# Message layer of a graph network: five of sixteen edge tiles gathered by TensorE instead of three, from a table in two fp16 parts

## The chip, the core and the metric

One NeuronCore of one Trainium2 chip runs the whole program. The metric is the device time in microseconds, the median of three runs. Work is spread over TensorE (PE), VectorE (DVE), ScalarE (ACT), GpSimd (POOL) and the queue of SyncE (SP), which only issues transfers.

## What is computed

Four graph layers over 3125 nodes of 96 features and 100,000 edges, with a layer norm before each later one. The change lies in the third, the message layer:

```python
src = edge_index[0]
dst = edge_index[1]
msg = jax.nn.relu(x[src] + edge_attr)
aggr = jax.ops.segment_sum(msg, dst, num_segments=x.shape[0])
h = x + aggr
h = jax.nn.relu(h @ W1 + b1) @ W2 + b2
return x + jax.nn.relu(h)
```

Edges are sorted by `dst`, and `edge_attr` here is an array of 100,000 x 96 floats. The first two layers work with a dense matrix of edge counts, the fourth (gated) layer gathers rows of 192 features for every edge.

## The kernel before

Edges are cut into tiles of 128 (`EP`), eight tiles (`GT`) to a group, 98 groups (`NG`). Node rows are held as 25 blocks (`NT`) of 125 nodes (`NP`). `message_layer` (L837) writes a program for each engine; the loops over groups are unrolled in it, and the engines meet at semaphores.

For each group the layer needs the 1024 source rows `x[src]` of 96 floats. They come in two ways.

- *By DMA.* POOL issues one indirect DMA for a tile (L931), which reads 128 rows of 384 bytes from the table `h_rows` into one of seven buffers (`RING`). It waits on `rows_free`, which DVE raises at the end of `make_onehots`.
- *By TensorE.* `picked_tiles` (L792) names the tiles that are left to it: one of an even group and two of an odd one, three of the sixteen of a pair. For such a tile DVE compares the 128 source ids, held in PSUM as f32 on 125 partitions, with the number of each node: one instruction of 25 x 128 elements (`make_picks`, L1007) makes a 0/1 matrix in bf16. `gather_rows` (L1130) multiplies it, in 25 matmuls that add up in PSUM, with the table `parts`, where each row of `h` stands as three bf16 parts (288 columns). `take_rows` (L1013) sums the three parts into the group's buffer. SP loads the ids (`load_row`), and ACT turns them into f32 (`widen`, L943).

When a group's rows are there, DVE adds the edge attributes, which SP loads into a ring of seven buffers (`add_edges`, L1036). ACT applies the ReLU in place (L958). DVE compares the destination ids with a stretch of 64 node numbers (`make_onehots`, L1057), and TensorE multiplies the eight tiles with these one-hot matrices in f32 (L1145). DVE adds the result to `aggT` (`add_total`, L1045). `group_steps` reads how many stretches a group has from a table that the kernel makes; there are 99 for the 98 groups.

The order on each engine is written out by hand. DVE, for a group g: `take_rows(g)`, `add_edges(g)`, `make_onehots(g)`, `make_picks(g + 2)`. TensorE: the sums of g, then `gather_rows(g + 2)`. ACT: the ReLU of g and, after an odd group, `widen` for the pair after next. SP: the edges of g and, after an even group, a row of ids for the pair after next. The gated layer (`gated_layer`, L1204) runs after it, with its own buffers and 784 indirect DMAs (L1269).

## Time and profile before

| | us |
|---|---|
| median of 3 runs | 3581.68 (3578.87 to 3584.29) |
| span of the profiled execution | 4069.9 |
| the profiled execution's own time | not given beside its span |
| message layer's loop in the profile | about 1600 to 2665 |
| gated layer's loop in the profile | about 2773 to 3963 |

Busy time over the span: PE 2792.4 us (69%), weight loads 1983.6 (49%), DVE 2233.5 (55%), POOL 1439.0 (35%), ACT 678.5 (17%). Times in the profile are us from the span's start; the span is 14% longer than the time of the runs. A group of lines gives busy time, the mean duration of one instruction in ns, and the idle time of the engine in front of it with what ended it; "issue" is idle time in which it waited for nothing that the profile shows, "remote" a releaser that it can't name.

### The profile page before, as it was taken

To read this page: it belongs to the slowest core of one execution; us is meant where nothing else is said; L and a number is where in the kernel's file an instruction comes from. 1 tells how busy PE (TensorE), PEld (TensorE's weight loads), DVE (VectorE), ACT (ScalarE), POOL (GpSimd) and SP (SyncE) were. 2 spreads that over 40 slices of the span, in tenths; PEclk is the share of its full clock that TensorE was granted. 3 is DMA by queue.
4 is the path that set the end of the run, shared out by engine and by line. 5 is a ranking of instruction groups with operands and counts; after the bars stand their busy time and mean duration, and the time that the engine had idled before them with its cause. 6 is when DMAs were issued, how large, how long until landed. Compare 5 with 4: busy or idle time off the path is not lost.

```text
span 4069.9 us, 59352 instructions
## 1 busy us (share of the span) xinstructions
PE 2792.4 (69%) x19895; PEld 1983.6 (49%) x19896; DVE 2233.5 (55%) x3813; ACT 678.5 (17%) x1120; POOL 1439.0 (35%) x1447
## 2 busy tenths in 40 slices
PE   3677779999998997577777777774244544454555
PEld 1211128999997775355555555552133323333333
DVE  6887777333346336476676676672244444444446
ACT  0234554000004001010010010011011111111111
POOL 0000000000000002565665665615566666667660
PEclk9999997999998998677777787775577666666766
DMA  0000000000000002222232232303222222222220
GB/s 24 0 0 0 0 0 3 2 2 2 2 2 4 1 1 54 64 78 72 76 78 74 73 78 75 84 12 85 66 79 75 75 76 74 73 74 78 75 73 16
DMA packets 109268, 180.96 MB, mean 44 GB/s; under 512 B 38949, under 2 KB 73287, under 8 KB 109049
## 3 DMA queue, kind: packets, MB, share of 16 engines
q0 software_dynamic: 58016, 108.47, 10.5%
q1 hardware_dynamic: 51033, 69.40, 6.1%
q8 instruction: 158, 2.59, 0.3%
q14 instruction: 61, 0.50, 0.0%
HBM read 172.96 MB, written 4.80 MB: 44 GB/s over the span
## 4 chain that ended last, share of the span: by engine, by line
PE 16%; another core or an unknown queue 15%; DVE 15%; issue 10%; ACT 1%; POOL 1%; DVEq 1%; DMA 1%; POOLq 0%
PE msg_sums L1130 10%; DVE msg_pick L1007 4%; PE msg_sums L1145 3%; DVE gate_rows L1331 3%; DVE gate_gated L1337 2%; DVE gate_gate L1340 1%; DVE gate_onehot L1365 1%; PE gate_sums L1429 1%; PE gate_sums L1440 1%; POOL gate_rows L1269 1%; DVE msg_rows L1036 1%; DVE msg_rows L1013 1%; DVE pre_aggT L1348 0%; DVEq L1356 0%
## 5 line engine op out<-in xcount | busy, mean ns | idle before, releaser
L1269 POOL DMA_INDIRECT gate_rows<-first_rows,all_src_i x784 | 774.7, 988 | 420.9 <-issue 232.0
L931 POOL DMA_INDIRECT msg_rows<-h_rows,all_src_i x637 | 642.7, 1009 | 423.6 <-DVEq L1060 247.6
L1130 PE MATMUL msg_sums<-msg_parts,msg_pick 125*128 125x288 bf16 x3675 | 622.9, 326 | 147.2 <-issue 133.9
L1440 PE MATMUL gate_sums<-gate_onehot,gate_passed 128*97 128x64 f32 x1584 | 223.9, 299 | 568.0 <-DVE gate_onehot L1367 290.4
L1130 PEld LDWEIGHTS msg_sums<-msg_parts,msg_pick 125*128 125x128 bf16 x3675 | 394.2, 111 | 351.3 <-issue 210.4
L919 POOL IOTA msg_node_no<- 125x25 f32 x1 | 0.2, 162 | 1588.9 <-POOLq L642 1588.9
L1331 DVE TENSOR_TENSOR gate_rows<-gate_rows,gate_sums 128x1536 f32<-128x1536 f32 x98 | 171.7, 1752 | 677.1 <-remote 500.4
L572 PE MATMUL hop_sums<-dense_work,dense_counts 125*128 125x192 f16 x6250 | 521.8, 247 | 14.3 <-DVE dense_t L526 6.6
L572 PEld LDWEIGHTS hop_sums<-dense_work,dense_counts 125*128 125x128 f16 x6250 | 519.1, 98 | 16.9 <-DVE dense_t L526 7.2
L1440 PEld LDWEIGHTS gate_sums<-gate_onehot,gate_passed 128*97 128x97 f32 x1584 | 206.9, 215 | 643.1 <-DVE gate_onehot L1367 354.9
L1007 DVE TENSOR_TENSOR msg_pick<-msg_sums,msg_node_no 125x3200 bf16<-125x3200 f32 x147 | 507.9, 3483 | 0.6 <-ACT msg_sums L943 0.3
L1429 PE MATMUL gate_sums<-pre_we,gate_edge 128*128 128x256 f32 (+1 forms) x784 | 373.5, 615 | 103.9 <-issue 94.1
L415 PE MATMUL cnt_sums<-cnt_hot,cnt_near 128*128 x1000 | 344.8, 406 | 121.4 <-DVE cnt_hot L354 116.4
L1145 PE MATMUL msg_sums<-msg_onehot,msg_rows 128*96 128x64 f32 x1584 | 224.2, 291 | 128.2 <-issue 120.6
L1429 PEld LDWEIGHTS gate_sums<-pre_we,gate_edge 128*128 128x128 f32 x784 | 181.8, 243 | 228.3 <-issue 209.3
L1145 PEld LDWEIGHTS msg_sums<-msg_onehot,msg_rows 128*96 128x96 f32 x1584 | 203.9, 205 | 159.8 <-issue 153.0
L415 PEld LDWEIGHTS cnt_sums<-cnt_hot,cnt_near 128*128 x1000 | 97.3, 97 | 363.3 <-issue 356.9
L1291 ACT ACTIVATE gate_gated<-gate_rows 128x768 f32<-128x768 f32 x98 | 82.7, 844 | 1018.7 <-DVE gate_rows L1331 603.1
L958 ACT ACTIVATE msg_rows<-msg_rows 128x768 f32<-128x768 f32 x98 | 82.6, 843 | 992.7 <-DVE msg_rows L1036 641.6
L352 DVE TENSOR_TENSOR cnt_near<-dense_work,cnt_src_n 128x256 f16 x500 | 180.3, 361 | 112.0 <-issue 87.9
L779 PE MATMUL conv_sums<-dense_work,dense_counts 125*128 125x288 bf16 x1875 | 236.3, 290 | 7.9 <-DVE dense_t L708 7.9
L1013 DVE TENSOR_REDUCE msg_rows<-msg_sums 128x96 f32<-128x288 f32 x147 | 64.5, 452 | 285.6 <-remote 273.6
(240 smaller groups left out, 2829.6 us busy)
## 6 DMA issues: line engine op xcount, KB each, us to landing
msg_edge<-edges SPq DMA_DIRECT2D x98, 384.0 KB
gate_edge<-edges SPq DMA_DIRECT2D x98, 128.0 KB
gate_rows<-first_rows,all_src_i POOLq DMA_INDIRECT x784
msg_rows<-h_rows,all_src_i POOLq DMA_INDIRECT x637
msg_src_row<-src_rows SPq DMA_DIRECT2D x49, 187.5 KB
first_rows<-pre_first SPq DMA_DIRECT2D x6, 375.0 KB
all_x<-x SPq DMA_DIRECT2D x1, 1171.9 KB
h_rows<-all_h SPq DMA_DIRECT2D x6, 187.5 KB
```

The lines of the kernel that those rows point to most:

```text
L352: nc.vector.tensor_tensor(nears.rearrange("p (c i) -> p c i", i=2), pairs2, low, ALU.is_equal)
L415: end_of_pair = nc.tensor.matmul(sums[:, b, 0:WIN * NT], nears.rearrange("p (c i) -> p i c", i=2)[:, i, :], hots[i], start=False, stop=Tru ...
L572: last = nc.tensor.matmul(sums[:, g0 + i, 0:2 * D], counts[0:NP, at:at + 128], half[frm][:, k, :], start=(k == 0), stop=(k == NT - 1))
L779: last = nc.tensor.matmul(sums[:, 4 * (q % 2) + i, 0:3 * D], counts[0:NP, at:at + 128], parts[:, j, :], start=(j == 0), stop=(j == NT - 1))
L931: nc.gpsimd.indirect_dma_start(out=rows[:, r, k, :], out_offset=None, in_=table, in_offset=bass.IndirectOffsetOnAxis(ap=src_i[:, at:at + 1 ...
L1007: nc.vector.tensor_tensor(pick[:, i % WIDE, :, :], source, spread(node_no[:, :], EP), ALU.is_equal).then_inc(picked, 1)
L1130: last = nc.tensor.matmul(got_rows[i % WIDE], pick[:, i % WIDE, j, :], parts[:, j, :], start=(j == 0), stop=(j == NT - 1))
L1145: last = nc.tensor.matmul(total[group % LAG], rows[:, group % RING, k, :], onehot[:, group % LAG, k, :], start=(k == 0), stop=(k == GT - 1))
L1269: nc.gpsimd.indirect_dma_start(out=rows[:, r, k, :], out_offset=None, in_=table, in_offset=bass.IndirectOffsetOnAxis(ap=src_i[:, at:at + 1 ...
L1331: nc.vector.tensor_tensor(to, to, products, ALU.add).then_inc(added, 1)
L1429: last = nc.tensor.matmul(sums[:, bank, to:to + end - frm], edge[:, group % SLOTS, half, :], we[:, frm:end], start=True, stop=True)
L1440: last = nc.tensor.matmul(total[group % LAG], passed[:, group % KEPT, k, :], onehot[:, group % LAG, k, :], start=(k == 0), stop=(k == GT - 1))
```

## The change

Five tiles of a pair are left to TensorE, two of the even group and three of the odd one. The ids are shifted by 1600 and kept in SBUF as fp16 (`src_near`), so that whole numbers up to 3125 fit exactly. The picks of a pair are made by 25 TENSOR_SCALAR instructions, one for each block of nodes, each for all 5 x 128 ids: 16 of them after an odd group, nine after the next even one. A pick is 1/4096 instead of 1, and the table holds two fp16 parts of 4096 h (192 columns). `take_rows` is gone: `add_edges` adds the edge attributes to the first part in PSUM, then to the tiles that came by DMA, then the second part. The edge ring has four buffers instead of seven. The picks share one space with `hT` and `first`, which are used after the loop, and with two tiles of the gated layer. On the host the table of ids is cut for five tiles.

```diff
-WIDE = 3
+PICKED = 5
+FIRST_HALF = 16
+EDGES = 4
+ROW_LIFT = 4096.0
+MIDDLE = 1600.0
...
@@ -792,8 +796,12 @@
 
 def picked_tiles(group):
 
-    first = group // 2 * WIDE
-    return [(first, GT - 1)] if group % 2 == 0 else [(first + 1, GT - 2), (first + 2, GT - 1)]
+    return [(0, GT - 2), (1, GT - 1)] if group % 2 == 0 else [(2, GT - 3), (3, GT - 2), (4, GT - 1)]
+
+
+def tiles_picked(groups):
+
+    return groups // 2 * PICKED + groups % 2 * 2
 
...
-        self.hT = m.sb("hT", [D, N], F32)
-        self.first = m.sb("first", [NP, 2, 4, 2 * D], F32)
+        space = m.sb("space", [EP, NT * PICKED * EP], F32)
+        self.pick = space[0:NP, :].bitcast(F16).rearrange("p (s t e) -> p s t e", s=2, t=NT)
+        self.hT = space[0:D, 0:N]
+        self.first = space[0:NP, 3136:3136 + 2 * 4 * 2 * D].rearrange("p (i n d) -> p i n d", i=2, n=4)
+        self.room = space[:, 4736:NT * PICKED * EP]
...
+        dst_f, iota, hT, first, pick = pre.dst_f, pre.iota, pre.hT, pre.first, pre.pick
...
-        edge = m.sb("edge", [EP, RING, GT, D], F32)
...
-        pick = m.sb("pick", [NP, WIDE, NT, EP], BF16)
-        parts = m.sb("parts", [NP, NT, 3 * D], BF16)
-        src_row = m.sb("src_row", [NP, 2, WIDE * EP], I32)
+        parts = m.sb("parts", [NP, NT, 2 * D], F16)
+        src_row = m.sb("src_row", [NP, 2, PICKED * EP], I32)
+        src_near = m.sb("src_near", [NP, 2, PICKED * EP], F16)
+        shift = m.sb("shift", [NP, 1], F32)
...
-        hid = m.sb("hid", [D, 2, 4 * NP], F32)
+        both = m.sb("both", [EP, 2 * 4 * NP], F32)
+        hid = both[0:D, :].rearrange("p (i w) -> p i w", i=2)
+        dst_i = both[:, 0:ET].bitcast(I32)
...
-        got_rows = [sums[:, 2 + i, 0:3 * D] for i in range(WIDE)]
-        wide = [sums[0:NP, b, 0:WIDE * EP] for b in (6, 7)]
+        got = [sums[:, 2, :].rearrange("p (i w) -> p i w", w=256),
+               sums[:, 3:5, :].rearrange("p b (i w) -> p (b i) w", w=256)]
...
-                r = group % RING
-                if group >= RING:
-                    sp.wait_ge(added, group - RING + 1)
+                r = group % EDGES
+                if group >= EDGES:
+                    sp.wait_ge(added, group - EDGES + 1)
+                    sp.wait_ge(placed, group - EDGES + 1)
                 sp.dma_start(edge[:, r, :, :].rearrange("p k d -> p (k d)"),
                              edges[group, :, :]).then_inc(edge_ready[r], 16)
...
-            nc.gpsimd.iota(node_no[:, :], [[NP, NT]], base=0, channel_multiplier=1,
+            nc.gpsimd.memset(shift[:, :], -MIDDLE).then_inc(numbered, 1)
+            nc.gpsimd.iota(node_no[:, :], [[NP, NT]], base=-int(MIDDLE), channel_multiplier=1,
                            allow_small_or_imprecise_dtypes=True).then_inc(numbered, 1)
...
@@ -939,12 +954,12 @@
             def widen(c):
                 act.wait_ge(row_loaded[c % 2], 16 * (c // 2 + 1))
                 if c >= 2:
-                    act.wait_ge(picked, WIDE * (c - 1))
-                nc.scalar.activation(wide[c % 2], src_row[:, c % 2, :], ACT.Copy).then_inc(widened, 1)
-            nc.scalar.activation(parts[:, :, 0:D], h[:, :, :], ACT.Copy).then_inc(rounded, 1)
+                    act.wait_ge(picked, NT * (c - 1))
+                nc.scalar.activation(src_near[:, c % 2, :], src_row[:, c % 2, :], ACT.Identity,
+                                     bias=shift[:, 0:1]).then_inc(widened, 1)
+            nc.scalar.activation(parts[:, :, 0:D], h[:, :, :], ACT.Copy, scale=ROW_LIFT).then_inc(rounded, 1)
+            act.wait_ge(numbered, 2)
             widen(0)
-            act.wait_ge(rest, 1)
-            nc.scalar.activation(parts[:, :, D:2 * D], t[:, :, :], ACT.Copy).then_inc(rounded, 1)
...
             for group in range(NG):
                 r = group % RING
                 act.wait_ge(added, group + 1)
+                act.wait_ge(placed, group + 1)
                 nc.scalar.activation(rows[:, r, :, :], rows[:, r, :, :], ACT.Relu).then_inc(sent, 1)
...
-            def make_picks(group):
-                c = group // 2
-                dve.wait_ge(widened, c + 1)
-                for i, k in picked_tiles(group):
-                    if i >= WIDE:
-                        dve.wait_ge(gathered, i - WIDE + 1)
-                    at = i % WIDE * EP
-                    source = wide[c % 2][:, at:at + EP].unsqueeze(1).to_broadcast([NP, NT, EP])
-                    nc.vector.tensor_tensor(pick[:, i % WIDE, :, :], source, spread(node_no[:, :], EP),
-                                            ALU.is_equal).then_inc(picked, 1)
-
-            def take_rows(group):
-                for i, k in picked_tiles(group):
-                    dve.wait_ge(gathered, i + 1)
-                    nc.vector.reduce_sum(rows[:, group % RING, k, :],
-                                         got_rows[i % WIDE].rearrange("p (a d) -> p d a", d=D), AX
-                                         ).then_inc(placed, 1)
+            def make_picks(c, j0, j1):
+                if j0 == 0:
+                    dve.wait_ge(widened, c + 1)
+                    if c >= 2:
+                        dve.wait_ge(gathered, PICKED * (c - 1))
+                for j in range(j0, j1):
+                    nc.vector.tensor_scalar(pick[:, c % 2, j, :], src_near[:, c % 2, :], node_no[:, j:j + 1],
+                                            1.0 / ROW_LIFT, ALU.is_equal, ALU.mult).then_inc(picked, 1)
 
             dve.wait_ge(rounded, 1)
-            nc.vector.tensor_tensor(t[:, :, :], h[:, :, :], parts[:, :, 0:D], ALU.subtract).then_inc(rest, 1)
-            dve.wait_ge(numbered, 1)
-            make_picks(0)
-            dve.wait_ge(rounded, 2)
-            nc.vector.tensor_tensor(parts[:, :, 2 * D:3 * D], t[:, :, :], parts[:, :, D:2 * D],
-                                    ALU.subtract).then_inc(split, 1)
-            make_picks(1)
+            nc.vector.scalar_tensor_tensor(out=parts[:, :, D:2 * D], in0=h[:, :, :], scalar=ROW_LIFT,
+                                           in1=parts[:, :, 0:D], op0=ALU.mult, op1=ALU.subtract).then_inc(split, 1)
+            dve.wait_ge(numbered, 2)
+            make_picks(0, 0, NT)
             dve.wait_ge(loaded, 80)
             dve.wait_ge(made, 2)
             link(nc.vector.tensor_copy(dst_f[:, :], dst_i[:, :]))
             dve.wait_ge(turned_out, len(GROUPS))
+            make_picks(1, 0, FIRST_HALF)
 
             def add_edges(group):
-                turn, r = divmod(group, RING)
-                dve.wait_ge(edge_ready[r], 16 * (turn + 1))
+                r, n = group % RING, len(picked_tiles(group))
+                k = GT - n
+                halves, of_edges = got[group % 2][:, 0:n, :], edge[:, group % EDGES, :, :]
+                dve.wait_ge(edge_ready[group % EDGES], 16 * (group // EDGES + 1))
+                dve.wait_ge(gathered, tiles_picked(group + 1))
+                nc.vector.tensor_tensor(rows[:, r, k:GT, :], halves[:, :, 0:D], of_edges[:, k:GT, :],
+                                        ALU.add).then_inc(half_placed, 1)
                 by_dma = sum(GT - len(picked_tiles(i)) for i in range(r, group + 1, RING))
                 dve.wait_ge(rows_ready[r], 16 * by_dma)
-                dve.wait_ge(placed, picked_tiles(group)[-1][0] + 1)
-                nc.vector.tensor_tensor(rows[:, r, :, :], rows[:, r, :, :], edge[:, r, :, :],
+                nc.vector.tensor_tensor(rows[:, r, 0:k, :], rows[:, r, 0:k, :], of_edges[:, 0:k, :],
                                         ALU.add).then_inc(added, 1)
+                dve.wait_ge(half_placed, group + 1)
+                nc.vector.tensor_tensor(rows[:, r, k:GT, :], rows[:, r, k:GT, :], halves[:, :, D:2 * D],
+                                        ALU.add).then_inc(placed, 1)
 
             def add_total(slot, nth):
 
@@ -1067,11 +1079,11 @@
                 dve.reg_mov(due[slot], 1)
                 link(nc.vector.memset(total[slot], 0.0))
             for group in range(NG):
-                take_rows(group)
                 add_edges(group)
                 steps = make_onehots(group)
-                if group + 2 < NG:
-                    make_picks(group + 2)
+                c, part = ((group + 3) // 2, (0, FIRST_HALF)) if group % 2 else (group // 2 + 1, (FIRST_HALF, NT))
+                if c < NG // 2:
+                    make_picks(c, *part)
             for i in range(LAG):
                 add_total((NG + i) % LAG, steps + (1 + i))
             dve.wait_ge(step_added, steps + (1 + LAG))
@@ -1122,13 +1134,14 @@
                 last.then_inc(turned, 1)
 
             def gather_rows(group):
-                for i, k in picked_tiles(group):
-                    pe.wait_ge(picked, i + 1)
-                    if i >= WIDE:
-                        pe.wait_ge(placed, i - WIDE + 1)
+                c = group // 2
+                pe.wait_ge(picked, NT * (c + 1))
+                if group >= 2:
+                    pe.wait_ge(placed, group - 1)
+                for n, (i, k) in enumerate(picked_tiles(group)):
                     for j in range(NT):
-                        last = nc.tensor.matmul(got_rows[i % WIDE], pick[:, i % WIDE, j, :], parts[:, j, :],
-                                                start=(j == 0), stop=(j == NT - 1))
+                        last = nc.tensor.matmul(got[group % 2][:, n, 0:2 * D], pick[:, c % 2, j, i * EP:(i + 1) * EP],
+                                                parts[:, j, :], start=(j == 0), stop=(j == NT - 1))
                     last.then_inc(gathered, 1)
 
             pe.wait_ge(turned_out, len(GROUPS))
@@ -1218,12 +1231,12 @@
         onehot = m.sb("onehot", [EP, LAG, GT, SPAN], F32)
         edge = m.sb("edge", [4 * DE, SLOTS, 2, EP], F32)
         passed = m.sb("passed", [EP, KEPT, GT, D + 1], F32)
-        gated = m.sb("gated", [EP, 2, GT, D], F32)
+        gated = pre.room[:, 0:2 * GT * D].rearrange("p (i k d) -> p i k d", i=2, k=GT)
         gate = m.sb("gate", [EP, 3, GT], F32)
         mw2T = m.sb("mw2T", [D, D + 1], F32)
         joint = m.sb("joint", [D + 1, D], F32)
         hid = m.sb("hid", [D, 2, 4 * NP], F32)
-        t = m.sb("t", [NP, NT, D], F32)
+        t = pre.room[0:NP, 2 * GT * D:2 * GT * D + NT * D].rearrange("p (t d) -> p t d", d=D)
         sums = m.ps("sums", [128, 8, BANK], F32)
         total = [sums[0:D + 1, b, 0:SPAN] for b in (6, 7)]
```

## Rows read from the trace of the kernel before

**Rows 1.** The head of the page.
```profile
span 4069.9 us, 59352 instructions
```

**Rows 2.** Windows: hops, convolutions, message loop, gated loop; columns as named in the first line.
```profile
core 0: us, PE busy (x) PEld busy (x) DVE busy (x) ACT busy (x) POOL busy (x), PEclk, DMA share, GB/s
680.00:1230.00 550.00, 535.58 (x6780) 532.91 (x6778) 197.65 (x358) 35.05 (x76) 0.00 (x0) 0.98 0.01 2
1300.00:1560.00 260.00, 239.49 (x1846) 189.79 (x1846) 94.73 (x179) 24.21 (x54) 0.00 (x0) 0.93 0.01 3
1620.00:2660.00 1040.00, 776.44 (x4927) 551.21 (x4926) 700.00 (x553) 95.16 (x138) 621.49 (x620) 0.77 0.29 74
2770.00:3950.00 1180.00, 539.85 (x2168) 351.61 (x2168) 468.72 (x543) 173.26 (x276) 764.25 (x773) 0.67 0.28 75
```

**Rows 3.** Groups of lines, shapes apart.
```profile
L1269 POOL DMA_INDIRECT gate_rows<-first_rows,all_src_i x784 | 774.7, 988 | 420.9 <-issue 232.0 <-ACT gate_passed L1294 184.0 <-DMA first_rows<-pre_first 4.9
L931 POOL DMA_INDIRECT msg_rows<-h_rows,all_src_i x637 | 642.7, 1009 | 423.6 <-DVEq L1060 247.6 <-issue 176.0
...
L572 PE MATMUL hop_sums<-dense_work,dense_counts 125*128 125x192 f16 x6250 | 521.8, 247 | 14.3 <-DVE dense_t L526 6.6 <-DVE dense_work L532 4.8 <-DVEq L516 2.8
...
L1007 DVE TENSOR_TENSOR msg_pick<-msg_sums,msg_node_no 125x3200 bf16<-125x3200 f32 x147 | 507.9, 3483 | 0.6 <-ACT msg_sums L943 0.3
```

**Rows 4.** DVE in order of time, one pair of groups: start, duration, idle time before.
```profile
2015.75 6.88 DVE L1007 TENSOR_TENSOR msg_pick<-msg_sums,msg_node_no 125x3200 bf16<-125x3200 f32 x2
2022.54 0.45 DVE L1013 TENSOR_REDUCE msg_rows<-msg_sums 128x96 f32<-128x288 f32 x1
2023.12 0.96 DVE L1036 TENSOR_TENSOR msg_rows<-msg_rows,msg_edge 128x768 f32<-128x768 f32 x1
...
2025.39 3.48 DVE L1007 TENSOR_TENSOR msg_pick<-msg_sums,msg_node_no 125x3200 bf16<-125x3200 f32 x1
2031.47 0.46 DVE L1013 TENSOR_REDUCE msg_rows<-msg_sums 128x96 f32<-128x288 f32 x1 [2.59 <-remote]
2034.46 0.46 DVE L1013 TENSOR_REDUCE msg_rows<-msg_sums 128x96 f32<-128x288 f32 x1 [2.53 <-remote]
2035.05 0.96 DVE L1036 TENSOR_TENSOR msg_rows<-msg_rows,msg_edge 128x768 f32<-128x768 f32 x1
...
2037.31 3.48 DVE L1007 TENSOR_TENSOR msg_pick<-msg_sums,msg_node_no 125x3200 bf16<-125x3200 f32 x1
```

**Rows 5.** POOL in order of time, in the same pair.
```profile
2021.96 0.95 POOL L931 DMA_INDIRECT msg_rows<-h_rows,all_src_i  x1 [0.31 <-issue]
2023.21 1.69 POOL L931 DMA_INDIRECT msg_rows<-h_rows,all_src_i  x1 [0.30 <-issue]
2025.32 0.97 POOL L931 DMA_INDIRECT msg_rows<-h_rows,all_src_i  x1 [0.41 <-issue]
```

**Rows 6.** TensorE in order of time, in the same pair.
```profile
2018.17 1.50 PE L1145 MATMUL msg_sums<-msg_onehot,msg_rows 128*96 128x64 f32 x16
2019.51 5.56 PE L1130 MATMUL msg_sums<-msg_parts,msg_pick 125*128 125x288 bf16 x43
...
2027.15 0.42 PE L1130 MATMUL msg_sums<-msg_parts,msg_pick 125*128 125x288 bf16 x2 [0.43 <-issue]
2028.58 0.40 PE L1130 MATMUL msg_sums<-msg_parts,msg_pick 125*128 125x288 bf16 x1 [1.02 <-issue]
```

**Rows 7.** DVE in order of time, in the counting stage.
```profile
607.13 0.34 DVE L354 TENSOR_SCALAR cnt_hot<-dense_work 128x500 f16 x1
607.39 0.34 DVE L360 TENSOR_SCALAR cnt_hot<-dense_work 128x500 f16 x1
```

**Rows 8.** DVE, then POOL, in order of time, at the end of the gated loop.
```profile
3968.64 6.21 DVE L1337 TENSOR_TENSOR gate_gated<-gate_gated,pre_gw 128x768 f32<-128x768 f32 x1
...
3968.77 5.25 POOL L1276 TENSOR_TENSOR all_x<-all_x,pre_shift 125x2400 f32<-125x2400 f32 x1
```

More of the change, by code:

```diff
@@ L842, in message_layer @@
         table, src_i = g["h_rows"], g["src_i"]
[L843 to L844 removed]
+        dst_f, iota, hT, first, pick = pre.dst_f, pre.iota, pre.hT, pre.first, pre.pick
         rows = m.sb("rows", [EP, RING, GT, D], F32)
[L846 removed]
+        edge = m.sb("edge", [EP, EDGES, GT, D], F32)
         onehot = m.sb("onehot", [EP, LAG, GT, SPAN], F32)
[L848 to L850 removed]
+        parts = m.sb("parts", [NP, NT, 2 * D], F16)
+        src_row = m.sb("src_row", [NP, 2, PICKED * EP], I32)
+        src_near = m.sb("src_near", [NP, 2, PICKED * EP], F16)
+        shift = m.sb("shift", [NP, 1], F32)
         node_no = m.sb("node_no", [NP, NT], F32)
@@ L865, in message_layer @@
         rows_ready = [m.sem(f"rows_ready{r}") for r in range(RING)]
-        edge_ready = [m.sem(f"edge_ready{r}") for r in range(RING)]
+        edge_ready = [m.sem(f"edge_ready{r}") for r in range(EDGES)]
         added = m.sem("added"); sent = m.sem("sent"); rows_free = m.sem("rows_free"); all_summed = m.sem("all_summed")
         numbered = m.sem("numbered"); row_loaded = [m.sem(f"row_loaded{i}") for i in range(2)]
-        widened = m.sem("widened"); rounded = m.sem("rounded"); rest = m.sem("rest"); split = m.sem("split")
-        picked = m.sem("picked"); gathered = m.sem("gathered"); placed = m.sem("placed")
+        widened = m.sem("widened"); rounded = m.sem("rounded"); split = m.sem("split")
+        picked = m.sem("picked"); half_placed = m.sem("half_placed"); gathered = m.sem("gathered"); placed = m.sem("placed")
         onehot_ready = m.sem("onehot_ready"); step_summed = m.sem("step_summed"); step_added = m.sem("step_added")
```

8 lines of the change are left out of this document (3 added, 5 removed).

## The prediction, made before the changed kernel was run

> **What bounds the kernel now.** I read the page's head first [rows 1]: the profiled span is 4069.9 us, while the runs shown have a median of 3581.68 us, so the profiled execution is 488.2 us, or 14%, longer than what is timed (its own time outside the profiler's span is not given). A sum of stalls taken straight from it would be wrong, so I asked which part of it is work that any execution must do. The windows [rows 2] place the stages: the hops and convolutions before 1560 us, the message layer's loop from about 1600 to 2665, the gated layer's loop from about 2773 to 3963.
>
> The groups of lines [rows 3] give the work. In the message loop POOL issues 637 row gathers: 642.7 us busy and 176.0 us of issue time between them, 818.7 us in all, or 1.285 us each. It also waits 247.6 us on DVE for buffers. In the gated loop the same sum is 774.7 + 232.0 = 1006.7 us, with 184.0 us of waits. The two waits come to 431.6 us, most of the 488.2 us by which the profile is too long. So I take it that in a timed run both loops run close to POOL's own pace, and that the profile's waits there are mostly the profile's.
>
> The chain inside one pair of groups says the same [rows 4 to 6]. A pair (DVE's double pick at 2015.75 to the next at 2037.31) lasts 21.56 us, and there are 49. DVE idles in it twice, 2.59 and 2.53 us, in front of the reductions of the odd group's picked rows, whose releaser is TensorE's gather. At that time TensorE waits for nothing that the profile names: after 43 matmuls in 5.56 us it runs one or two at a time with 0.3 to 1.0 us between them ("issue"). Without the two waits DVE's pair is 21.56 - 5.12 = **16.4 us**. POOL's pair is 13 gathers at 1.25 us (start to start) plus 0.75 us, the excess of the one that took 1.69 instead of 0.95 us: **17.0 us**. TensorE's, at full rate, is 75 gathers of 288 columns and 32 f32 matmuls. I take 0.122 us for the first, from 2.4 GHz and the hop's 521.8 / 6250 = 0.083 us for 192 columns (0.083 x 288/192 = 0.125, rounded down for the clock of 0.98), and 1.50 / 16 = 0.094 for the second: 9.2 + 3.0 = **12.2 us**. So POOL sets the pair now by a little, DVE stands 0.6 us behind it, and the loop takes about 49 x 17.0 = 833 us in a timed run.
>
> **The change part by part, for one pair.**
> - *Gathers moved from POOL to TensorE.* Five tiles of sixteen instead of three: 11 gathers instead of 13, 2 x 1.25 = 2.5 us off POOL. POOL's pair: 17.0 - 2.5 = **14.5 us** (539 gathers instead of 637).
> - *TensorE's gathers.* 5 x 25 = 125 matmuls of 192 fp16 columns instead of 75 of 288. The nearest row has this very shape, the hop's 125x192 f16 with 125x128 weights [rows 3]: 0.083 us. 125 x 0.083 + 3.0 = **13.4 us** at full rate. At the message window's clock of 0.77 [rows 2] it is 17.4 us.
> - *Picks.* Three TENSOR_TENSORs of 3200 elements, 3.40 us start to start (6.88 for two, less the overlap) = 10.2 us, become 25 TENSOR_SCALARs of 640 fp16 elements. The nearest rows are the counting stage's TENSOR_SCALARs, 500 elements in fp16 [rows 7]: 0.34 us long but 0.26 us from start to start. 3200 elements in 3.40 us is 0.94 per ns; 500 at that rate would be 0.53 us, so this form moves several elements a cycle. Four at 0.96 GHz make 0.13 us of the 0.26, and 640 need 0.04 more: 0.30 us, 7.4 us a pair. Upper bound: 0.38 each by duration, 9.5 us. Below: 0.26 each, 6.5 us. I take 7.4, since picks follow each other without a wait. Saved: 2.8 us (0.7 to 3.7).
> - *Placing and adding.* Out: three reductions at 0.45 and two adds at 0.96, 3.27 us. In: per group an add of the picked tiles from PSUM, an add of the tiles from DMA, and a second add from PSUM. A TENSOR_TENSOR here costs its elements over 0.96 GHz plus about 0.15 us (768: 0.96; 3200: 3.48), so even groups take 0.35 + 0.75 + 0.35 and odd ones 0.45 + 0.65 + 0.45: 3.0 us. Saved: 0.3 us. The third add waits for the first alone, which is then two instructions old: nothing. Queued behind both are the onehots and the next picks.
> - *DVE's pair:* 16.4 - 2.8 - 0.3 = **13.3 us** (12.4 to 15.4).
> - *When the picks come.* TensorE's gather of an even group now waits for a whole chunk of 25; of these nine (2.7 us) stand behind that group's onehots, where one pick of 3.48 us stood. Odd groups find theirs ready. No later than now, so nothing. If DVE becomes late, this wait shows first.
> - *ACT* waits for the third add before its ReLU (0.4 us later) and converts 640 ids instead of 384 per pair. It is busy 95 us of 1040 [rows 2], so its own time is hidden; the 0.4 us stands in front of the sums, which TensorE reaches after a gather of 4 to 6 us. Nothing while that holds.
> - *SP.* The edge ring of four instead of seven: SP's queue also holds, behind every even group's load, the next row of ids, which waits for ACT's conversion three groups back. So loads were already issued about four groups ahead. Nothing; two groups are 15 us of cover, and DMA is busy 0.29 of the time.
> - *Start and end.* Before the loop DVE makes two passes over the table (2400 elements, 2.65 us by the formula above) and three picks of 3.4: 15.5 us. Then it will be one pass, 25 picks and 16 of the second chunk, 2.65 + 7.4 + 4.7 = 14.8 us. Nothing. Sharing one space among picks, hT, first and the gated layer's tiles adds no wait, since their uses are already ordered.
>
> **What they cost each other.** POOL's gather at 2023.21 took 1.69 us, and DVE's add of two SBUF operands ran beside it from 2023.12 to 2024.08; gathers beside picks, which read the ids from PSUM, took 0.95 [rows 4, 5]. POOL is held there until DVE ends. In the other direction DVE's 0.96 us product took 6.21 us beside POOL's 5.25 us sum [rows 8]. The new picks read and write SBUF alone, in the fast form, during half of the pair. Bounds: nothing, or POOL kept out of all 7.4 us. I take a gather that starts inside a pick as held for half a pick, 0.17 us: 11 x 0.5 x 0.17 = **0.9 us**. The nearest row bears that out: a hold lasts until the DVE instruction in progress ends, and these are short.
> This is where a page speaks against the change. The Trainium skill, SBUF — State Buffer, section "SBUF: two separate sides", says that DVE in its two-port modes and GpSimd take one port pair by turns, exclusively, and that GpSimd then can't write descriptors. The rows of 1.69 and 6.21 us agree that there is such a hold; none has POOL beside a pick of the fast form.
>
> **Sum.** The pair's bound is POOL, 14.5 + 0.9 = 15.4 us, with DVE at 13.3 and TensorE at 13.4 at full rate. 17.0 - 15.4 = 1.6 us, x 49 = 78 us. Against the median: 3581.7 - 78 = **about 3504 us**. The profiled span itself may fall less or even rise, since TensorE has 314 instructions a pair to be fed where it has 214, and the stall of [rows 6] grows with them.
>
> **The rivals.**
> - *POOL and the picks exclude each other for whole runs (slower).* Place: POOL's gathers during DVE's runs of 9 and 16 picks. For it: the two holds above, and picks that leave no gap (start to start below their duration). Against it: each pick is an instruction of its own. Price: POOL's pair is 14.5 + 7.4 = 21.9 us, 4.9 more than now, x 49 = +240: about 3820 us. It decides from the point at which POOL loses 2.5 us a pair, a third of the picks' time.
> - *TensorE becomes the bound (no change or a little slower).* 17.4 us at the clock of 0.77, 0.4 over today's pair: 3600 us. For it: the clock of that window. Against it: the granted clock goes with how busy TensorE was, 0.98 and 0.93 in the windows where it was busy 97% and 92%, 0.77 at 75%, 0.67 at 46% [rows 2]; at 13.4 of 15.4 us it would be busy 87%, the clock near 0.9 and the pair 14.9 us.
> - *TensorE's feed is short in timed runs too (slower).* If the "issue" gaps belong to its instructions and not to the profiling, DVE waits for it now and waits longer: 5.1 us x 314/214 = 7.5, with 15.4 about 23 against 21.6: +1.3 x 49, 3645 us. Against it: then the profile would not be 488 us longer than the runs.
> - *The fast form fails at 640 elements with two operations.* At 0.94 a ns, 25 x 0.75 = 18.8 us instead of 10.2: DVE's pair is 24.7, +7.7 x 49, 3960 us. Against it: [rows 7].
> - *No cost between DVE and POOL:* 14.5 us a pair, 3581.7 - 122 = 3459 us; a gain of this side with a loop now longer than 833 us reaches 3430.
>
> **How the numbers follow.** The forecast with the case of no contention has 0.66. Exclusion 0.15, TensorE's clock 0.08 (half of it within 0.2% of now), feed 0.06, the slow form 0.03, and 0.02 for a loss elsewhere that just cancels the gain. Faster by over 0.2%: 0.68 (the forecast and a quarter of the clock's case). Within 0.2% (7 us, about what a measurement of this kernel can tell from no change): 0.06 (half of the clock's case and the 0.02). Slower: 0.26 (the rest). Range: from 3425, below the case without contention, to 3650, which holds TensorE's clock and the feed; full exclusion and the slow form stay outside. The forecast's own range is 3430 to 3560.
>
> **What would show it.** TENSOR_SCALAR of 640 elements 0.35 to 0.40 us long, 0.30 from start to start; POOL's gathers above 0.95 us only beside picks, mean below 1.2; DVE's message-loop work at 13.3 us a pair without waits; TensorE's clock above 0.85. Gathers of a mean above 1.5 us, or picks far above 0.4 us, mean the exclusion. A DVE that waits in front of its first add for gathers of 192 columns, with TensorE busy over 90%, means that TensorE is the bound.

## The result, and the profile after

The changed kernel takes **3451.1 us** (median of 4 runs, 3449.09 to 3453.87) against 3582.98 us of the kernel before (4 runs). The ratio is 0.963, interval 0.9615 to 0.9644: 131.9 us faster. The forecast was 3504 us with 3425 to 3650, so the direction and the range held, and the gain was 1.7 times the 78 us that were foreseen.

The first profile of the kernel before [rows 1] was taken in an execution 14% longer than the timed ones; a second one below agrees with them, and where before and after are compared in us from here on, it stands for before. The profiled execution of the changed kernel took 3451.4 us, with a span of 3449.7.

Windows of the changed kernel: hops, convolutions, message loop, gated loop. The first line names the columns of all windows shown.

```profile
core 0: us, PE busy (x) PEld busy (x) DVE busy (x) ACT busy (x) POOL busy (x), PEclk, DMA share, GB/s
684.00:1230.00 546.00, 530.86 (x6584) 528.11 (x6581) 193.76 (x349) 32.01 (x69) 0.00 (x0) 0.98 0.01 2
1300.00:1560.00 260.00, 237.74 (x1856) 188.91 (x1857) 95.98 (x182) 23.61 (x53) 0.00 (x0) 0.94 0.01 3
1620.00:2290.00 670.00, 633.59 (x7442) 623.56 (x7441) 584.28 (x1653) 113.91 (x142) 512.82 (x516) 0.99 0.49 117
2380.00:3360.00 980.00, 635.23 (x2261) 430.11 (x2259) 493.45 (x568) 179.96 (x287) 745.00 (x771) 0.72 0.33 91
```

Its groups of lines, which answer to [rows 3] (line numbers are 13 to 15 higher), with TensorE's gather beside the hop of the same shape:

```profile
L1282 POOL DMA_INDIRECT gate_rows<-first_rows,all_src_i x784 | 757.6, 966 | 243.8 <-issue 238.7 <-DMA first_rows<-pre_space 5.1
L946 POOL DMA_INDIRECT msg_rows<-h_rows,all_src_i x539 | 537.3, 997 | 164.1 <-issue 163.5 <-DVEq L1072 0.6
L1143 PE MATMUL msg_sums<-msg_parts,pre_space 125*128 125x192 f16 x6125 | 531.9, 249 | 36.3 <-DVE pre_space L1021 36.3
L576 PE MATMUL hop_sums<-dense_work,dense_counts 125*128 125x192 f16 x6250 | 521.9, 247 | 14.3 <-DVE dense_t L530 6.7 <-DVE dense_work L536 4.8 <-DVEq L520 2.8
...
L1021 DVE TENSOR_SCALAR pre_space<-msg_src_near,msg_node_no 125x640 f16<-125x640 f16 x1225 | 393.9, 395 | 11.9 <-ACT msg_src_near L958 11.5
```

POOL's gathers in the message loop need 537.3 us and 163.5 of issue time, and for other engines they wait 0.6 us in all. The two come to 700.8 us, 14.3 a pair: an engine that waits for nobody sets the pace. TensorE is busy 633.6 of 670 us (13.5 us a pair) at a clock of 0.99, DVE 584.3, and both wait a little for others. The gated loop is untouched and POOL's alone too: 757.6 + 238.7 = 996.3 us.

DVE in order of time, one pair of the changed kernel, the answer to [rows 4]:

```profile
2001.74 0.44 DVE L1041 TENSOR_TENSOR msg_rows<-msg_sums,msg_edge 128x288 f32<-128x288 f32 x1
2002.11 0.64 DVE L1045 TENSOR_TENSOR msg_rows<-msg_rows,msg_edge 128x480 f32<-128x480 f32 x1
2002.68 0.44 DVE L1048 TENSOR_TENSOR msg_rows<-msg_rows,msg_sums 128x288 f32<-128x288 f32 x1
...
2003.86 0.69 DVE L1069 TENSOR_TENSOR msg_onehot<-pre_iota,pre_dst_f 128x512 f32<-128x512 f32 x1
2004.81 5.06 DVE L1021 TENSOR_SCALAR pre_space<-msg_src_near,msg_node_no 125x640 f16<-125x640 f16 x16 [0.26 <-ACT msg_src_near L958]
2009.79 0.34 DVE L1041 TENSOR_TENSOR msg_rows<-msg_sums,msg_edge 128x192 f32<-128x192 f32 x1
2010.52 0.76 DVE L1045 TENSOR_TENSOR msg_rows<-msg_rows,msg_edge 128x576 f32<-128x576 f32 x1 [0.38 <-DMA msg_rows<-h_rows,all_src_i]
```

POOL in the same pair, the answer to [rows 5]:

```profile
2004.19 1.17 POOL L946 DMA_INDIRECT msg_rows<-h_rows,all_src_i  x1 [0.30 <-issue]
2005.67 0.95 POOL L946 DMA_INDIRECT msg_rows<-h_rows,all_src_i  x1 [0.30 <-issue]
2006.93 0.95 POOL L946 DMA_INDIRECT msg_rows<-h_rows,all_src_i  x1 [0.30 <-issue]
2008.18 0.95 POOL L946 DMA_INDIRECT msg_rows<-h_rows,all_src_i  x1 [0.30 <-issue]
...
2010.70 1.40 POOL L946 DMA_INDIRECT msg_rows<-h_rows,all_src_i  x1 [0.30 <-issue]
```

Three gathers stand inside the run of 16 comparisons (2004.81 to 2009.87) at 0.95 us each, as if DVE were idle. The two long ones are 0.22 and 0.45 us longer; the one-hot comparison beside the first had 0.36 us to run when it began (until 2004.55), the add beside the second 0.58 (until 2011.28). Both excesses are that rest less 0.13 us, as if the gather needed something that DVE holds 0.13 us after its start and waited there until DVE's instruction ended. The whole trace follows this: 67 gathers began inside such an add or one-hot comparison that had run for at least 0.05 us and had more than 0.13 us to go, and 66 of them were longer by that rest less 0.13 us, to within 0.01 us. The adds with one operand in PSUM (L1041, L1048) never did this: 55 gathers had one beside them 0.12 us after their start and took 0.943 to 0.952 us. So DVE's instructions with two SBUF operands held POOL, and the new picks hardly did.

The picks weren't free, though: DVE paid. Among the comparisons beside two of these gathers the longest took 453 ns, where the median is 375:

```profile
L1021 DVE TENSOR_SCALAR pre_space<-msg_src_near,msg_node_no x11: 368/375/453, 2004.8 to 2008.0; 125x640 f16<-125x640 f16 x11
```

(minimum, median and maximum in ns, first and last start). Of the 243 gathers of the trace that meet comparisons alone, the median is 0.950 us and the longest comparison beside one of them takes 0.452 us in the median. So gather and comparison do wait for each other, and here it was mostly DVE, which has time to spare.

### The profile page after: what moved, and what is told of

It is laid out like the page before. It is cut to its first block, busy times and chain, and to the rows that moved or that the text cites. A ratio compares the mean times of both kernels' runs of the same rounds, so it can differ in the third digit from the quotient of the medians.

```text
span 3449.7 us, 65375 instructions
## 1 busy us (share of the span) xinstructions
PE 2703.8 (78%) x22345; PEld 2109.0 (61%) x22346; DVE 2096.9 (61%) x4939; ACT 692.8 (20%) x1119; POOL 1316.5 (38%) x1350
## 4 chain that ended last, share of the span: by engine, by line
POOL 34%; issue 11%; DVE 5%; PE 2%; DMA 1%; ACT 0%; DVEq 0%; POOLq 0%; ACTq 0%
POOL gate_rows L1282 22%; POOL msg_rows L946 12%; DVE pre_space L1021 2%; PE msg_sums L1143 1%; DVE msg_rows L1045 0%; DMA first_rows<-pre_space 0%; PE gate_sums L1453 0%; ACT msg_src_near L958 0%; DVE pre_space L1350 0%; DVE msg_rows L1041 0%; DMA msg_rows<-h_rows,all_src_i 0%; DMA msg_src_row<-src_rows 0%; PE msg_sums L1158 0%; DVE pre_space L1113 0%; DMA gate_rows<-first_rows,all_src_i 0%
## 5 line engine op out<-in xcount | busy, mean ns | idle before, releaser
L1282 POOL DMA_INDIRECT gate_rows<-first_rows,all_src_i x784 | 757.6, 966 | 243.8 <-issue 238.7
L946 POOL DMA_INDIRECT msg_rows<-h_rows,all_src_i x539 | 537.3, 997 | 164.1 <-issue 163.5
L1143 PE MATMUL msg_sums<-msg_parts,pre_space 125*128 125x192 f16 x6125 | 531.9, 249 | 36.3 <-DVE pre_space L1021 36.3
L1143 PEld LDWEIGHTS msg_sums<-msg_parts,pre_space 125*128 125x128 f16 x6125 | 513.0, 99 | 43.4 <-DVE pre_space L1021 37.8
L576 PE MATMUL hop_sums<-dense_work,dense_counts 125*128 125x192 f16 x6250 | 521.9, 247 | 14.3 <-DVE dense_t L530 6.7
L1442 PE MATMUL gate_sums<-pre_we,gate_edge 128*128 128x256 f32 (+1 forms) x784 | 419.7, 702 | 14.1 <-DVE gate_rows L1344 10.4
L1021 DVE TENSOR_SCALAR pre_space<-msg_src_near,msg_node_no 125x640 f16<-125x640 f16 x1225 | 393.9, 395 | 11.9 <-ACT msg_src_near L958 11.5
L1442 PEld LDWEIGHTS gate_sums<-pre_we,gate_edge 128*128 128x128 f32 x784 | 220.4, 296 | 140.1 <-issue 110.8
L1304 ACT ACTIVATE pre_space<-gate_rows 128x768 f32<-128x768 f32 x98 | 82.6, 843 | 794.6 <-DVE gate_rows L1344 794.6
L530 DVE TENSOR_REDUCE dense_t<-hop_sums 125x384 f32<-125x768 f32 (+1 forms) x63 | 54.9, 871 | 292.9 <-PE hop_sums L576 292.9
L236 ACT ACTIVATE dense_work<-cnt_key,cnt_start_at 128x786 f32<-128x786 f32 x158 | 150.2, 951 | 387.1 <-PE cnt_sums L419 341.2
L783 PEld LDWEIGHTS conv_sums<-dense_work,dense_counts 125*128 125x128 f16 x1875 | 185.7, 99 | 57.4 <-DVE dense_t L712 8.6
```

Of the source, the lines that this page charges most:

```text
L236: nc.scalar.activation(own[:, j % 2, :], key[:, :], ACT.Identity, bias=start_at[:, bass.ds(w, 1)]).then_inc(shifted, 1)
L576: last = nc.tensor.matmul(sums[:, g0 + i, 0:2 * D], counts[0:NP, at:at + 128], half[frm][:, k, :], start=(k == 0), stop=(k == NT - 1))
L783: last = nc.tensor.matmul(sums[:, 4 * (q % 2) + i, 0:3 * D], counts[0:NP, at:at + 128], parts[:, j, :], start=(j == 0), stop=(j == NT - 1))
L946: nc.gpsimd.indirect_dma_start(out=rows[:, r, k, :], out_offset=None, in_=table, in_offset=bass.IndirectOffsetOnAxis(ap=src_i[:, at:at + 1 ...
L1021: nc.vector.tensor_scalar(pick[:, c % 2, j, :], src_near[:, c % 2, :], node_no[:, j:j + 1], 1.0 / ROW_LIFT, ALU.is_equal, ALU.mult).then_i ...
L1143: last = nc.tensor.matmul(got[group % 2][:, n, 0:2 * D], pick[:, c % 2, j, i * EP:(i + 1) * EP], parts[:, j, :], start=(j == 0), stop=(j = ...
```

## The experiments

Unless told otherwise, each is an edit of the changed kernel; the ratio is to the kernel before.

### The kernel before, a second time

No edit; one run.

> The kernel before, unchanged, for a second profile. Theory A (POOL paces both loops when nothing disturbs the execution): the span is about 3580 us; the message loop's 637 gathers take about 833 us from first to last (17.0 us a pair), the gated loop's 784 about 1000; TensorE's matmuls no longer stand one by one with gaps of 0.3 to 1.0 us. Rival B (TensorE's gaps belong to the kernel): the gaps are there again, the message loop's gathers span over 900 us, and DVE waits over 2 us a pair in front of the odd group's reductions.

3585.21 us. Windows of its message and gated loops, then two of its groups of lines, then POOL's gathers by their line (min, median, max in ns, first and last start):

```profile
1620.00:2420.00 800.00, 647.64 (x5029) 497.64 (x5029) 706.80 (x565) 97.24 (x141) 614.49 (x609) 0.92 0.38 96
2530.00:3500.00 970.00, 637.68 (x2267) 431.73 (x2265) 493.48 (x569) 178.77 (x286) 736.92 (x765) 0.72 0.33 91
```

```profile
L931 POOL DMA_INDIRECT msg_rows<-h_rows,all_src_i x637 | 645.7, 1014 | 194.0 <-issue 193.7 <-DVEq L1060 0.3
L1130 PE MATMUL msg_sums<-msg_parts,msg_pick 125*128 125x288 bf16 x3675 | 532.1, 309 | 141.8 <-DVE msg_pick L1007 141.2 <-ACT msg_aggT L950 0.6
```

```profile
L931 POOL DMA_INDIRECT msg_rows<-h_rows,all_src_i x637: 940/944/2709, 1596.8 to 2435.4; - x160
```

POOL's wait of 247.6 us in [rows 3] is 0.3 here, and its gathers span 1596.8 to 2435.4, 838.5 us, 17.1 us a pair, where the prediction had 17.0. TensorE no longer stands in front of single matmuls as in [rows 6]:

```profile
1999.90 7.69 PE L1130 MATMUL msg_sums<-msg_parts,msg_pick 125*128 125x288 bf16 x50 [1.83 <-DVE msg_pick L1007]
2009.57 3.24 PE L1130 MATMUL msg_sums<-msg_parts,msg_pick 125*128 125x288 bf16 x25 [0.64 <-DVE msg_pick L1007]
```

What it waits for is DVE's picks, 141.2 us. Rival B falls: the gaps belonged to that one execution. Their cause isn't known. The changed kernel's gathers span 1596.4 to 2296.8 (last section), 700.4 us; the difference, 138 us, is the whole gain of 132 us within 6. Most of the six is behind the message loop: in the changed kernel's trace the way from its last gather to the gated layer's first is 2.4 us longer, and the gated layer's gathers span 2.8 us more.

### Three tiles in the new form

```diff
-PICKED = 5
+PICKED = 3
...
-    return [(0, GT - 2), (1, GT - 1)] if group % 2 == 0 else [(2, GT - 3), (3, GT - 2), (4, GT - 1)]
+    return [(0, GT - 1)] if group % 2 == 0 else [(1, GT - 2), (2, GT - 1)]
```

(and the count of tiles and the host's table of ids, likewise)

> The changed kernel with three of sixteen tiles left to TensorE, as before, in the new form (fp16 parts, 25 comparisons). Theory A (only the number of POOL's gathers matters): 13 gathers a pair at 1.30 us, 16.9 us against 14.3 us, 49 x 2.6 = +127 us over the changed kernel: 3578 us, within 10 us of the kernel before. Rival C (the cheaper picks are what pays, DVE paced the loop): DVE's pair falls by some 5 us against before, and the time is near or below 3451 us.

3580.27 us (10 runs), ratio 0.9994 [0.9985, 1.0004]: no change against the kernel before. Its window of the loop and what DVE waited for in it:

```profile
1620.00:2420.00 800.00, 580.32 (x5042) 542.36 (x5039) 493.13 (x1645) 102.96 (x141) 613.92 (x611) 0.81 0.38 96
```

```profile
DVE msg_rows L1045 <- DMA msg_rows<-h_rows,all_src_i: 259.5, 94, 4.0
```

DVE has 214 us less to do in this window than in the kernel before (493.1 against 706.8) and spends them waiting for gathered rows to land. Cheaper picks alone are worth nothing here, and with five tiles instead of three the same form is 129 us faster. Rival C falls.

The equal times hide an exchange, however. POOL's 637 gathers take 42 us over the undisturbed 0.947 us each, as they do in the kernel before, but by other causes. There the adds cost it 27 us and the one-hot comparisons 13; here they cost 10 and 6, and the picks of 384 elements some 26. Two gathers beside such picks in one pair, and one before the loop's steady part with DVE beside it:

```profile
2001.16 1.04 POOL L946 DMA_INDIRECT msg_rows<-h_rows,all_src_i  x1 [0.30 <-issue]
2002.51 1.07 POOL L946 DMA_INDIRECT msg_rows<-h_rows,all_src_i  x1 [0.30 <-issue]
```

```profile
1598.57 5.83 DVE L1021 TENSOR_SCALAR pre_space<-msg_src_near,msg_node_no 125x384 f16<-125x384 f16 x25 [0.75 <-ACT msg_src_near L958]
1600.47 4.52 POOL L946 DMA_INDIRECT msg_rows<-h_rows,all_src_i  x1 [0.30 <-issue]
1604.31 0.57 DVE L1031 CAST pre_dst_f<-msg_both 128x784 f32<-128x784 int32 x1
```

The last is what the prediction's rival of whole runs describes: a gather that ends only when a run of 25 picks and the copy behind it have passed. It is the only one among the 637. So picks of this form can hold POOL, and the 0.95 us beside those of 640 elements isn't a property of the form alone.

### No picks after the second chunk

```diff
-                for j in range(j0, j1):
+                if c >= 2:
+                    dve.sem_inc(picked, j1 - j0)
+                for j in range(j0, j1) if c < 2 else ():
```

> The changed kernel, but the comparisons are made for the first two chunks only; later gathers of TensorE read stale picks, so the picked rows are wrong from the third pair on. DVE loses 7.9 us of work in each 14.3 us pair. Theory A (POOL paces, and a pick of the fast form holds it for almost nothing): 3440 to 3451 us; the 256 gathers that stood beside picks keep 0.95 us. Rival D (picks hold POOL): the gathers fall from a mean of 0.997 to 0.95 and the time by more than 25 us. Rival C (DVE paces): it falls by 50 us or more.

3459.48 us (3458.42 to 3460.61), outside the 3440 to 3451 that I had expected and 8 us *slower* than with all picks. DVE's load falls by 367 us in the same window, and the loop gets no shorter:

```profile
1620.00:2290.00 670.00, 630.32 (x7381) 620.61 (x7379) 216.87 (x475) 112.21 (x140) 515.17 (x509) 0.98 0.48 116
```

```profile
L946 POOL DMA_INDIRECT msg_rows<-h_rows,all_src_i x539 | 546.7, 1014 | 164.1 <-issue 162.0 <-DVEq L1074 2.1
```

POOL's gathers are 9.4 us longer in all (546.7 against 537.3), which is the loss. A DVE without picks waits for rows, and then does its adds and one-hot comparisons at other moments of POOL's rhythm, where more gathers meet them: in this trace 135 gathers had one of the two beside them 0.12 us after their start and took 1.17 (adds) and 1.25 us (comparisons) in the mean, against some 111 at 1.14 and 1.15 in the changed kernel. Rivals C and D fall for this kernel: neither DVE's load nor its picks of 640 elements set the time.

### Fewer gathers by POOL

```diff
+def by_dma(group):
+    return GT - len(picked_tiles(group)) - (group >= 2 * RING)
...
-                for k in range(GT - len(picked_tiles(group))):
+                for k in range(by_dma(group)):
```

(and the count that DVE waits for, likewise)

> The changed kernel, but from the fifteenth group on POOL leaves out one gather in each group; that tile's rows are the stale ones of the buffer. 84 gathers of 539 go. POOL's pair would be 9 x 1.30 = 11.7 us against 14.3. Theory A with TensorE next (13.4 to 13.6 us a pair with its waits): 42 pairs x 0.8 = 34 us less, about 3417 us, with TensorE busy over 97% of the loop. Rival E (DVE is next, at 13.3 plus its holds): the same time but TensorE with idle time that ends at DVE's picks. Rival C or any theory in which POOL doesn't pace: no change.

3426.38 us (3423.24 to 3427.63), 25 us less than the changed kernel. The window, and POOL's waits in it:

```profile
1620.00:2260.00 640.00, 622.78 (x7439) 616.52 (x7436) 576.26 (x1648) 113.90 (x142) 428.62 (x442) 1.00 0.48 117
```

```profile
POOL msg_rows L951 <- issue: 118.6, 378, 3.6
POOL msg_rows L951 <- DVEq L1077: 85.8, 63, 2.3
```

POOL now waits 85.8 us for buffers, and TensorE is busy 97% of the stretch. The 84 gathers left out would be worth 84 x 1.25 = 105 us if POOL still set the pace. So TensorE stands right behind POOL, and all that is left in the changed kernel's loop in front of it is about 25 us. The expected 34 us took TensorE's pair at 13.5; with its waits it is 13.7 (25 us over 42 pairs are 0.6 us less than 14.3).

### The destination ids in PSUM

```diff
+        dst_near = sums[:, 6:8, :].rearrange("p b w -> p (b w)")[:, 0:ET]
...
+            link(nc.vector.tensor_copy(dst_near, dst_i[:, :]))
...
-                    targets = dst_f[:, group * GT:(group + 1) * GT].unsqueeze(2).to_broadcast([EP, GT, SPAN])
+                    targets = dst_near[:, group * GT:(group + 1) * GT].unsqueeze(2).to_broadcast([EP, GT, SPAN])
```

> The changed kernel, but the message layer's one-hot comparison reads the destination ids from PSUM instead of SBUF (one more copy of 784 ids before the loop, about 1 us), so it has one SBUF operand instead of two. Theory A': what holds POOL in this loop are DVE instructions with two SBUF operands, 26.9 us in all over 539 gathers, of which 70 gathers beside this comparison carry 0.21 us each, 14.8 us: the gathers beside it fall to 0.95 us and the time by 8 to 15 us, to 3436 to 3443. Rival D (it is DVE's activity or its writes that hold POOL, not the second SBUF operand): the gathers stay at 1.16 us and the time at 3451.

3435.25 us (5 runs), ratio 0.9583 [0.957, 0.9596], 16 us faster than the changed kernel (whose interval is 0.9615 to 0.9644) and the fastest here that does the layer's whole work. Its groups of lines:

```profile
L947 POOL DMA_INDIRECT msg_rows<-h_rows,all_src_i x539 | 529.4, 982 | 164.2 <-issue 163.5 <-DVEq L1074 0.6
...
L1071 DVE TENSOR_TENSOR msg_onehot<-pre_iota,msg_sums 128x512 f32<-128x512 f32 x99 | 68.1, 688 | 14.6 <-issue 0.7
```

POOL in order of time beside this comparison, which ran from 2003.65 to 2004.34 there:

```profile
2003.99 0.95 POOL L947 DMA_INDIRECT msg_rows<-h_rows,all_src_i  x1 [0.31 <-issue]
2005.24 0.95 POOL L947 DMA_INDIRECT msg_rows<-h_rows,all_src_i  x1 [0.30 <-issue]
```

In this trace 65 gathers had the comparison beside them 0.12 us after their start, all at 0.943 to 0.967 us; in the changed kernel some 70 had a mean of 1.15. Where the changed kernel's rule, the rest less 0.13 us, would have made 46 of them longer by 0.32 us in the median, nothing is added. The comparison itself is about as long as before (688 against 708 ns). Moving one operand out of SBUF removed the hold.

The time is shown less fully. The profiled execution took 3449.37 us, 2 us less than the changed kernel's; the other four took 3430.78 to 3435.42 and have no trace. In the profiled one the one-hot comparisons' 14.8 us are gone, but the adds met POOL at other moments and cost 14.4 us instead of 7.7: the loop is 8 us shorter, and it starts 5 us later. Where the rest of the 16 us comes from isn't shown.

### Six tiles

```diff
-PICKED = 5
+PICKED = 6
...
-EDGES = 4
+EDGES = 3
```

(and three tiles in each group, with their places in PSUM and the host's table, and the last stage's tile `t` in the shared space)

> The changed kernel with six of sixteen tiles left to TensorE, three in each group, comparisons of 768 ids, an edge ring of three and the layer's last-stage tile in the shared space (so that it fits). POOL's pair is 10 x 1.30 = 13.0 us. Theory A with TensorE next: 150 x 0.083 + 32 x 0.085 = 15.2 us a pair and 0.3 of waits, 15.5 against 14.3: 49 x 1.2 = +59 us over the changed kernel, about 3510 us, POOL waiting for buffers, TensorE busy over 97% of the loop. Rival C (more of the same helps as long as POOL has gathers): about 3390 us. Rival E (DVE next, 25 x 0.33 = 8.3 plus 5.9 = 14.2 us): about 3450 us.

3502.06 us (3499.67 to 3504.33), 51 us slower than five tiles. The window, and POOL's waits:

```profile
1620.00:2330.00 710.00, 710.00 (x8591) 710.00 (x8589) 612.97 (x1648) 118.27 (x142) 479.16 (x476) 1.00 0.45 112
```

```profile
POOL msg_rows L946 <- issue: 122.2, 401, 0.3
POOL msg_rows L946 <- DVEq L1072: 102.1, 74, 2.8
```

TensorE has no idle time at all; its 150 gathers and 32 sums a pair at the full clock are the bound: 8591 matmuls in 710 us are 0.083 us each, 15.0 us for the 182 of a pair. So of the three counts tried, three and five tiles leave POOL as the bound and six makes it TensorE; five stands just before they meet.

### The kernel before with an edge ring of four

```diff
-        edge = m.sb("edge", [EP, RING, GT, D], F32)
+        edge = m.sb("edge", [EP, 4, GT, D], F32)
...
-                if group >= RING:
-                    sp.wait_ge(added, group - RING + 1)
+                if group >= 4:
+                    sp.wait_ge(added, group - 3)
```

(and the buffer's number in `add_edges`, likewise)

> The kernel before with the edge ring of four buffers instead of seven, alone. All theories that I hold: no change, 3575 to 3590 us, since SP's queue already waits for ACT's conversion three groups back. Rival F (the ring is a cost that the changed kernel pays and its gain hides): slower by over 0.2%, and DVE waits for edges in front of its add.

3584.08 us (10 runs), ratio 1.0003 [0.9994, 1.0012]. The smaller ring costs this kernel nothing, and in the changed kernel's loop too DVE has no wait for edges. Rival F falls.

### The ids as f32

```diff
-        src_near = m.sb("src_near", [NP, 2, PICKED * EP], F16)
+        src_near = m.sb("src_near", [NP, 2, PICKED * EP], F32)
```

> The changed kernel with the shifted ids in SBUF as f32 instead of fp16; the picks are written as fp16 as before. The comparisons leave the form in which all operands are of 16 bits. If they then move one element a cycle, 25 x (0.67 + 0.13) = 20 us a pair and DVE's pair is about 26 us: DVE paces, 49 x 12 = +590 us, 4040 us. If two a cycle, 25 x 0.46 = 11.5 us, DVE's pair 17.4 us, 49 x 3.1 = +150 us, about 3600 us, slower than the kernel before: the gain of moving tiles then depends on the form. Theory A' expects POOL's gathers beside these comparisons at 0.95 us in either case; rival D expects them held.

3631.01 us (3630.37 to 3632.4), ratio 1.0133 [1.0118, 1.0149]: slower than the kernel before. Groups of lines and the loop's window:

```profile
L1021 DVE TENSOR_SCALAR pre_space<-msg_src_near,msg_node_no 125x640 f16<-125x640 f32 x1225 | 598.0, 562 | 13.4 <-ACT msg_src_near L958 13.3
L946 POOL DMA_INDIRECT msg_rows<-h_rows,all_src_i x539 | 577.9, 1072 | 272.6 <-issue 138.8 <-DVEq L1072 133.8
```

```profile
1620.00:2400.00 780.00, 652.86 (x6908) 634.96 (x6906) 721.22 (x1539) 105.83 (x132) 528.52 (x495) 0.89 0.40 95
```

From start to start a comparison takes 0.463 us instead of 0.296, as expected of half the speed. A pair then lasts 17.3 us (849.4 us of gathers' span over 49); DVE is busy 92% of the window and waits there for nobody longer than 0.3 us at a time, POOL waits for it 133.8 us, and the change as a whole loses. Theory A' fails on POOL's gathers: beside these comparisons their median is 1.107 us, not 0.95. They are held, as rival D has it, but by 0.16 us and not to the end of a run.

## Why the prediction was right, and what it missed

**What bounds the kernel before** was right: POOL, 17.0 us a pair, 833 us for the loop; the second profile has 17.1 and 838.5. Setting the first profile's waits aside, from the balance of 431.6 against 488.2 us, is borne out by it. With the waits left in, DVE would have seemed to wait for TensorE, and the change would have looked like a loss. The engines behind POOL were sized less well. DVE was put at 16.4 us a pair and has 15.1 of work (706.8 of 800 us), TensorE at 12.2 and is busy 13.8: its gathers of 288 columns take 7.69 us for 50 and 3.24 for 25 in the pair above, where the prediction had 0.122 us each. Neither changes the forecast, since neither was the bound.

**The terms.** Gathers moved: 1.25 us each without a hold (0.947 and 0.30 of issue), as foreseen; between the runs with three and with five tiles 129 us over 98 gathers are 1.32 each, since their share of holds went with them. TensorE's gather: 0.083 us foreseen, and 0.082 to 0.083 from start to start; 13.4 us a pair against 13.5 busy. Picks: 0.30 us from start to start foreseen, 0.296 the median, but 16 and 9 take 5.06 and 2.89 us in the pair above, so 25 take 7.9 instead of 7.4, since some comparisons are stretched to 0.45 us beside a gather. DVE's pair: 13.3 foreseen, 12.5 busy. The edge ring, ACT and SP: nothing, as said.

**The step that was off** is the term of what DVE and POOL cost each other. The prediction had 0.75 us a pair from adds with two SBUF operands and 0.9 us from picks, 1.65 in all. From the rows, 537.3 us less 539 gathers at the undisturbed 0.947 leaves 26.9 us, 0.55 a pair. The difference, 1.1 us a pair, times 49 is 54 us, the size of the 53 by which 3504 was too high; the loop before, 5 us longer than foreseen, and the 6 us lost elsewhere cancel.

- *The picks* were the larger error. The gathers that meet comparisons and nothing else have a median of 0.950 us and a mean of 0.957; all gathers with a pick beside them 0.12 us after their start come to 2.5 us over the undisturbed, 0.05 a pair where I had put 0.9. Part of this is luck. With 384 and 768 elements the same form cost POOL some 22 (without the gather of 4.52 us) and 21 us, 0.45 and 0.43 a pair, half of my figure; at 640 it is DVE's comparison that waits. The reasoning, a hold for a part of one short instruction, was sound, but it left open which of the two waits.
- *The adds and one-hot comparisons.* Adds cost 0.16 us a pair instead of 0.75, and the one-hot comparisons, which also read two SBUF operands and which the prediction put at nothing, cost 0.30. What each costs depends on when it meets a gather. The adds are shorter than before (0.64 and 0.76 us instead of 0.96), but whether that is the reason isn't shown: with the ids in PSUM the same adds cost 0.29.
- *The signs named beforehand* held for the comparison's length, the gathers' mean of 0.997 us and the clock. One was the wrong way round: the gathers above 0.95 us stand beside adds and one-hot comparisons, not beside picks.

**The rule on the port pair.** The Trainium skill, SBUF — State Buffer, section "SBUF: two separate sides", has DVE's two-port modes and GpSimd exclude each other for a whole instruction, the loser fully blocked. That is one instruction; the rival at 3820 us took it for whole runs of 9 and 16, which is more than the page says. One gather of 4.52 us, in the run with three tiles, looks like that; in the changed kernel the longest that meets comparisons alone is 1.095 us. Within one gather of 0.95 us three comparisons begin, so the gather doesn't hold DVE off for its whole length either. What the runs mostly show is a wait of a part of one comparison, paid by POOL (0.16 us in the median with f32 ids) or by DVE (0.08 us at 640 elements).

The same section has two SBUF operands against a GpSimd instruction that reads SBUF as a second case. The rows of 1.69 and 6.21 us that the prediction set beside the two-port rule belong here, for their DVE instructions add or multiply two SBUF operands. The runs agree with it: a hold until DVE's instruction ends, which vanished when one operand moved to PSUM.

**The rivals.** TensorE's granted clock was 0.99 with TensorE busy 95% of the loop, against 0.92 with 81% in the kernel before; with three tiles in the new form and 73% it was 0.81. So the bound by TensorE was near (25 us away) but at the full clock. The feed rival fell with the second profile. The slow form was not met; the f32 run shows what half the speed would have cost.

## What to carry to other kernels

Find the engine that waits for nobody and count its instructions. As long as that was POOL, its gathers came every 1.29 to 1.32 us from start to start in every kernel here, while taking 63% of DVE's work away gave nothing. Once another engine is the bound (the runs with fewer gathers, with six tiles and with f32 ids), the count no longer gives the time. An engine off the path is then worth loading up to the point at which it has no idle time, and that point can be computed from the shape's own row. Before trusting a stall in a profile, set its span beside the timed runs; where they differ by 14%, take a second profile.

## What the runs showed of the hardware

- A DVE comparison with a per-partition scalar, from start to start (medians): 0.229 us for 384 fp16 elements, 0.296 for 640, 0.329 for 768, 0.463 for 640 with f32 input. The three fp16 figures lie on 0.129 us and 3.84 elements a ns; with the same fixed part the f32 figure gives 1.92 a ns.
- A gather of 128 rows issued by POOL takes 0.947 us alone. It waits for a DVE instruction with two SBUF operands that is still running 0.13 us after its start, until that ends (66 of 67 gathers of the changed kernel to within 0.01 us); with one operand in PSUM it doesn't. A DVE instruction that begins at about the gather's start is itself stretched instead: one-hot comparisons to 0.75 us from 0.69.
- Beside the comparisons above, the gather's median was 0.950 us (640 fp16), 1.017 (768 fp16) and 1.107 (640 with f32 input). With 384 elements it had two values: 0.944 us where a comparison was stretched to 0.53 us from 0.31, and 1.04 where none was; one gather of 4.52 us lasted to the end of a whole run. At 640 a comparison that began 0.65 us into the gather was stretched, at 768 none was and the gather was longer. So each can wait for the other, and the traces suggest that the phase decides which; no run was made to show that. These three lines are of POOL's gather in the changed kernel, with six tiles and with f32 ids: min, median and max in ns.

```profile
L946 POOL DMA_INDIRECT msg_rows<-h_rows,all_src_i x539: 943/950/2678, 1596.4 to 2296.8; - x180
```

```profile
L946 POOL DMA_INDIRECT msg_rows<-h_rows,all_src_i x490: 943/1016/2673, 1598.8 to 2319.7; - x164
```

```profile
L946 POOL DMA_INDIRECT msg_rows<-h_rows,all_src_i x539: 940/1105/2676, 1598.3 to 2447.7; - x180
```

- What the holds by two SBUF operands cost depends on phase: the same adds and one-hot comparisons cost POOL 22.5 us with the picks between them and 35.4 without.
